# Self-attention of a decoder layer: VectorE turns 32x32 blocks and a round trip through DRAM places them, instead of TensorE transposes; GpSimd forms low halves; scores run two items ahead

## What is computed

```python
k = jnp.einsum('ihd,bpd->biph', W_K, x)
q = jnp.einsum('ihd,bpd->biph', W_Q, x)
v = jnp.einsum('ihd,bpd->biph', W_V, x)
scores = jnp.einsum('biph,biqh->biqp', k, q)
mask = jnp.tril(jnp.ones((pos, pos), dtype=x.dtype))
masked = scores * mask - jnp.float32(10000000000.0) * (1.0 - mask)
attn = jax.nn.softmax(masked / jnp.sqrt(jnp.float32(d_head)), axis=-1)
z = jnp.einsum('biqp,biph->biqh', attn, v)
z_flat = jnp.transpose(z, (0, 2, 1, 3)).reshape(b, pos, -1)
out = jnp.einsum('df,bqf->bqd', W_O, z_flat)
...
xq = activation_quant(rms_norm(x))
g = jax.nn.silu(ternary_matmul(xq, W_g))
u = ternary_matmul(xq, W_u)
p = g * u
return ternary_matmul(p, W_d)
```

## Time and profile before

| | us |
|---|---|
| median of 3 runs | 1622.2 |
| lowest, highest | 1622.14, 1622.71 |
| span of the profiled execution | 1621.2 |
| TensorE busy | 1574.0 (97%) |
| TensorE weight load busy | 1270.9 (78%) |
| VectorE busy | 1014.8 (63%) |
| ScalarE busy | 788.7 (49%) |
| GpSimd busy | 286.4 (18%) |

### The profile page before, as it was taken

One profiled execution on the slowest core, in us unless ns is written; L12 is line 12 of the kernel. 1 busy time (PEld: TensorE's weight loads), 2 busy tenths in 40 slices (PEclk: granted clock), 3 DMA queues, 4 the chain that ended last, 5 costly groups with the idle time before them and its releaser, 6 DMA issues. The chain is left out here.

```text
span 1621.2 us, 25726 instructions
## 1 busy us (share of the span) xinstructions
PE 1574.0 (97%) x8332; PEld 1270.9 (78%) x8352; DVE 1014.8 (63%) x2125; ACT 788.7 (49%) x1789; POOL 286.4 (18%) x301
## 2 busy tenths in 40 slices
PE   8999999999999999999999999997999998999997
PEld 7888888888888888888888888885887775565564
DVE  4555555555555555555555555567899996877854
ACT  5444444444444444444444444444888875433332
POOL 0000000000000000000000000004788872433432
PEclk9999999999999999999999999997999999999998
DMA  5000010100101001010010100011111100000000
GB/s 175 29 31 19 26 32 14 44 19 26 32 13 45 19 26 32 13 42 22 26 32 13 32 32 26 2 45 47 52 58 59 40 20 1 1 27 1 26 26 27
DMA packets 40393, 50.85 MB, mean 31 GB/s; under 512 B 3488, under 2 KB 19872, under 8 KB 40352
## 3 DMA queue, kind: packets, MB, share of 16 engines
q1 hardware_dynamic: 40352, 50.35, 9.7%
HBM read 46.14 MB, written 4.19 MB: 31 GB/s over the span
## 5 line engine op out<-in xcount | busy, mean ns | idle before, releaser
L162 POOL TENSOR_TENSOR norm_rstd<-norm_var_eps,minus_half 128x4 f32<-128x4 f32 x12 | 12.2, 1014 | 1116.2 <-DVE norm_var_eps L122 1116.2
L645 DVE SCALAR_TENSOR_TENSOR acc<-attn_bank,prob_recip,acc 128x512 f32<-128x512 f32 x256 | 179.7, 744 | 16.9 <-PE attn_bank L487 16.9
L510 ACT ACTIVATE probs<-probs,neg_max 128x128 f32<-128x128 f32 (+3 forms) x256 | 142.0, 557 | 61.7 <-DVE neg_max L590 61.7
L581 DVE TENSOR_TENSOR zT_lo<-attn_bank,zT_hi 128x512 fp32r<-128x512 f32 x64 | 44.3, 692 | 190.0 <-ACT zT_hi L504 190.0
L504 ACT CAST kT_hi<-attn_bank 128x512 fp32r<-128x512 f32 x64 | 37.5, 587 | 180.3 <-PE attn_bank L355 180.3
L581 DVE TENSOR_TENSOR qT_lo<-attn_bank,qT_hi 128x512 fp32r<-128x512 f32 x64 | 44.2, 691 | 126.0 <-ACT qT_hi L504 125.9
L581 DVE TENSOR_TENSOR kT_lo<-attn_bank,kT_hi 128x512 fp32r<-128x512 f32 x64 | 44.3, 692 | 122.9 <-ACT kT_hi L504 122.9
L1195 PE MATMUL y_bank<-wdT_f32r,prod_hi 128*128 128x512 f32 x256 | 110.8, 433 | 3.0 <-POOL prod_lo L1136 2.5
L1136 POOL TENSOR_TENSOR prod_lo<-prod,prod_hi 128x512 fp32r<-128x512 f32 x64 | 85.6, 1337 | 142.1 <-ACT prod_hi L1244 142.1
L590 DVE CUSTOM_DVE_ANT_0 probs<-attn_bank,mask 128x128 f32<-128x128 f32 (+3 forms) x256 | 109.8, 485 | 0.1
L487 PE MATMUL attn_bank<-woT_hi,zT_hi 128*128 128x512 f32 x256 | 106.2, 415 | 1.6 <-DVE zT_lo L581 1.4
(11 more groups left out here) (149 smaller groups left out, 4176.1 us busy)
## 6 DMA issues: line engine op xcount, KB each, us to landing
rows_twice<-in_ctx_dram SPq DMA_DIRECT2D x64, 128.0 KB, 2.6
rows<-in_L_attn_W_K_dram SPq DMA_DIRECT2D x16, 256.0 KB, 2.6
rows<-in_L_attn_W_Q_dram SPq DMA_DIRECT2D x16, 256.0 KB, 2.9
rows<-in_L_attn_W_V_dram SPq DMA_DIRECT2D x16, 256.0 KB, 3.4
rows<-in_L_attn_W_O_dram SPq DMA_DIRECT2D x16, 256.0 KB, 2.7
rows_twice<-in_L_ffn_W_g_dram SPq DMA_DIRECT2D x16, 256.0 KB, 2.7
rows_twice<-in_L_ffn_W_u_dram SPq DMA_DIRECT2D x16, 256.0 KB, 2.8
rows_twice<-in_L_ffn_W_d_dram SPq DMA_DIRECT2D x16, 256.0 KB, 2.7
```

What stands on the lines that cost most here:

```text
L510: nc.scalar.activation(probs[:, cols], probs[:, cols], ACT.Exp, bias=low[:, par, t:t + 1], scale=-1.0, accum_out=total[:, par, t:t + 1]).t ...
L581: nc.vector.tensor_tensor(parts[1][:, at:at + cols], bank[:, 0:cols], parts[0][:, at:at + cols].bitcast(F32), ALU.subtract).then_inc(done, 1)
L645: nc.vector.scalar_tensor_tensor(out=acc[:, b * NT + t, :], in0=O_BANK[t][:], scalar=recip[:, par, t:t + 1], in1=acc[:, b * NT + t, :], op ...
```

## The change

TensorE transposes nothing but x at the start. Weights are loaded so that their 32x32 blocks lie already at the right place, and VectorE turns each block (`nc.vector.transpose`, which transposes within 32x32 blocks). For the probabilities and v it turns blocks from SBUF or PSUM into the tile `turned` of 128 x 1792 values (ten blocks of probabilities, four of v). SP stores this tile in a DRAM scratch and loads it again by four DMAs, one for each group of 32 partitions, straight into `pv_lo`; ScalarE casts that to `pv_hi`, and GpSimd subtracts in place. GpSimd also makes the weights' low halves. k, q, scores, mask and v's turn run two items ahead of z and the output (`AHEAD`). The signs go to DRAM and are loaded again in the two later stages, for which the SBUF was taken by the new tiles. x and the quantised x are read by TensorE with a stride of four columns (`chunk_of`).

```diff
+    E, R = 4, 32
+    AHEAD = 2
+    NBLK = NT * (NT + 1) // 2 + NT
+    V_AT = (7, 10, 11, 13)
+    PIECES = ((0, 8), (8, NBLK))
...
+        scratch = [nc.dram_tensor(f"turned_scratch{i}", (P, NBLK, E, R), F32).ap() for i in range(2)]
...
             @block.sync
             def _(sp):
+                def bounce(i, par, first):
+
+                    sp.wait_ge(p_turn, i + 1)
+                    sp.dma_start(scratch[par].rearrange("p n c s -> p (n c s)"), turned[:]).then_inc(written, 16)
+                    sp.wait_ge(written, i * 16 + 16)
+                    if not first:
+                        sp.wait_ge(z_full, i)
+                    for c in range(E):
+                        sp.dma_start(pv[1][c * R:(c + 1) * R, :].bitcast(F32).rearrange("r (n a s) -> r n a s", a=E, s=R),
+                                     scratch[par][:, :, c, :].rearrange("(a r) n s -> r n a s", a=E)).then_inc(landed, 16)
...
+                def step(h, b, last):
+                    if not (last and b == B - 1):
+                        bounce(h * B + b + 1, (b + 1) % 2, False)
+                    if b > 0:
+                        keep_signs(h, b - 1)
+                    if b == 0 and not last:
+                        load_projection(sp, "wk", wk, h + 1)
+                        load_projection(sp, "wq", wq, h + 1)
+                    if b == 1:
+                        wait_apart(sp, k, f_turn, h * 3 + 1)
+                        load_down(sp, h)
+                        if not last:
+                            load_projection(sp, "wv", wv, h + 1)
+                            load_output(sp, h + 1)
...
             @block.gpsimd
             def _(pool):
-                for n in range(B - 2):
-                    norm_gpsimd(nc, pool, norm, k.minus_half, n)
...
+                def pieces_lo(i):
+                    for g, (first, end) in enumerate(PIECES):
+                        cols = slice(first * P, end * P)
+                        pool.wait_ge(pv_hi, i * len(PIECES) + (g + 1))
+                        nc.gpsimd.tensor_tensor(pv[1][:, cols], pv[1][:, cols].bitcast(F32), pv[0][:, cols].bitcast(F32),
+                                                ALU.subtract).then_inc(pv_lo, 1)
...
             @block.scalar
             def _(act):
...
+                def pieces_hi(i):
+                    act.wait_ge(landed, i * (16 * E) + 16 * E)
+                    for first, end in PIECES:
+                        cols = slice(first * P, end * P)
+                        nc.scalar.copy(pv[0][:, cols], pv[1][:, cols].bitcast(F32)).then_inc(pv_hi, 1)
...
                 def step(h, b, last):
-                    more = not (last and b == B - 1)
                     i = h * B + b
...
+                    more = not (last and b + AHEAD >= B)
+                    if not (last and b == B - 1):
+                        exps(i + 1, (b + 1) % 2)
                     if more:
...
+                    if not (last and b == B - 1):
+                        pieces_hi(i + 1)
...
             @block.vector
             def _(dve):
...
+                def turn_probs(i):
+                    for t in range(NT):
+                        dve.wait_ge(exp_done, i * NT + (t + 1))
+                        last = nc.vector.transpose(blocks(turned[:], t, 3, t + 1),
+                                                   blocks(probs[:, s_at[t]:s_at[t] + (t + 1) * P], 0, 1, t + 1))
+                    last.then_inc(p_turn, 1)
+
+                def turn_v(i, first):
+
+                    dve.wait_ge(v_full, i + 1)
+                    if not first:
+                        dve.wait_ge(written, i * 16)
+                    nc.vector.transpose(blocks(turned[:], V_AT[0], V_AT[1] - V_AT[0], 2), blocks(v_bank[:], 0, 1, 2))
+                    nc.vector.transpose(blocks(turned[:], V_AT[2], V_AT[3] - V_AT[2], 2), blocks(v_bank[:], 2, 1, 2)).then_inc(v_turn, 1)
...
                 def step(h, b, last):
-                    more = not (last and b == B - 1)
                     i = h * B + b
                     par = b % 2
+                    more = not (last and b + AHEAD >= B)
+                    if not (last and b == B - 1):
+                        turn_probs(i + 1)
...
+                    if more:
+                        turn_v(i + AHEAD, False)
+                        rows_of_scores(i + AHEAD, par)
```

More of the change, by code:

```diff
@@ L162, in norm_gpsimd, with attention @@
     nc.gpsimd.tensor_tensor(norm.rstd[:], norm.var[:], minus_half[:], ALU.pow).then_inc(norm.rstd_ready, 1)
-def attention(nc, x_in, wk, wq, wv, wo, wg, wu, wd, acc, wT_ffn, rows, k, norm):
-    wd_v = wd.rearrange("(c p) f -> p c f", p=P)
-    gT, uT, dT = wT_ffn
+def attention(nc, x_in, wk, wq, wv, wo, wg, wu, wd, acc, signs, rows, k, norm):
     x_v = x_in.rearrange("b (t p) d -> p (b t) d", p=P)
[L174 to L208, removed]
+    E, R = 4, 32
+    AHEAD = 2
+    ITEMS = H * B
+    BEGIN = ["x0", "x1", "x2", "x3", "k0", "x4", "q0", "x5", "v0", "x6", "x7", "s0",
+             "k1", "x8", "x9", "q1", "x10", "x11", "v1", "x12", "x13", "s1", "x14", "x15"]
     s_at = [sum(P * (u + 1) for u in range(t)) for t in range(NT)]
-    pt_at = [sum(P * (NT - u) for u in range(j)) for j in range(NT)]
     NPAIR = P * NT * (NT + 1) // 2
-    S_BANK = [(0, 0), (0, P), (1, 0), (2, 0)]
-    PT_GROUPS = [(0,), (1,), (2, 3)]
+    NBLK = NT * (NT + 1) // 2 + NT
+    V_AT = (7, 10, 11, 13)
+    PIECES = ((0, 8), (8, NBLK))
     with ExitStack() as ctx:
@@ new lines, in turn_views, with turn_weight @@
+                def turn_views(out, x, chunked):
+                    if not chunked:
+                        return out, x
+                    return out.rearrange("p (a c s) -> p a c s", a=E, c=NC), x.rearrange("p (a r c) -> p a c r", a=E, c=NC)
+                def turn_weight(name, n):
+                    other, before = BEFORE_IN_TMP[name]
+                    if not (isinstance(n, int) and n + before == 1):
+                        dve.wait_ge(w_lo[other], n - 1 + before)
+                    dve.wait_ge(w_loaded[name], n * (16 * E))
+                    nc.vector.transpose(*turn_views(w_turned[TMP[name]][:], raw[name][:], name != "wo")).then_inc(w_turn[name], 1)
@@ L751, in _ @@
             def _(sp):
+                signs.load(sp)
                 def step(b, h):
@@ L1122, in _ @@
             def _(sp):
+                for t in range(NHT):
+                    sp.dma_start(wdT[:, t * D:(t + 1) * D].bitcast(F32), signs.d[:, t * D:(t + 1) * D]).then_inc(wd_loaded[t], 16)
                 with sp.Fori(0, B - 1) as b:
```

606 lines of the change are left out of this document (297 added, 309 removed).

## The result

The changed kernel takes 1761.0 us (1758.5 to 1762.4), the kernel before in the same comparison 1622.2: a ratio of 1.086, interval [1.085, 1.088]. It is 139 us slower. The forecast was 1809 us, the range 1600 to 2050.

What follows compares the result with a forecast made beforehand. The prediction took the detour's chain to bound self-attention, not TensorE: 63 periods of 19.5 us (1228.5), with start, first loads, tail and weights 1297.7, plus 510.6 for later stages and 1.0 to the median: 1809 us, range 1600 to 2050.

Steps and rivals of the forecast that it cites:

- One ring: Self-attention's chain per item: casts of landed blocks, exponentials, last turn, store, four loads; period 19.5 us against TensorE's 14.9.
- Its pieces: Per item: casts 1.8, exponentials 2.3, turn 0.7, store 4.1, load latency 1.8, packets 8.5, hand-offs 0.3 us.
- t: Price of one 128 B packet in the detour's loads, 448 per engine an item: taken as 18.9 ns.
- a line and a flat price: Bounds on a 128 B packet's price: 9.6 ns by a line through 512 B and 2 KB packets, 28.1 ns if flat.
- the sign turns: Packet price of 12.8 ns, a period of 16.7 us, where the time equals that of the kernel before.
- the loads overrun by 0.7 us: Down, value and output weights behind the detour's loads need 5.7 us in a 5.0 us gap: 10 us over 15 heads.
- I leave the start as it is: Item 0's scores were to end at 29.4 us as before, since turning the first weights replaces their transposes.
- The sum: First store's end 35.9, loads 10.3, 63 periods 1228.5, tail 13.0, weights 10, later stages 510.6: 1808.3 us.
- TensorE's clock: Falls to half while TensorE waits at z, returns within the item; rival that it stays low: near 2460 us, chance 0.04.
- The single buffer: The one buffer for landed blocks is free 1.9 us before the next loads want it.
- The DMA share: Busy share of the DMA engines in self-attention, expected near 60% if the forecast was right.
- Cheap packets: Rival: 128 B packets at 9.6 ns, period 15.3 us, time 1531 us, faster than before; chance 0.18.

Runs made afterwards that it cites:

- e11: e3's kernel with one more store of the same 896 KB, to another scratch, written before the loads are issued: 1920.2 us, ratio 1.186.
- e4: Changed kernel with the four loads reading each partition's 7 KB in one run, the placing of blocks left out: 1605.9 us, ratio 0.991 to the kernel before.
- e8: Changed kernel with one load of 128 partitions in 7 KB runs in place of four loads, placing left out: 1552.7 us (one run), ratio 0.958.
- e7: Changed kernel with VectorE instead of GpSimd forming the low halves of the landed blocks: 1789.7 us, ratio 1.104 to the kernel before.
- e3: Changed kernel with v's weights of the next head loaded one item earlier (b = 0): 1688.5 us, ratio 1.041 to the kernel before.
- e1: Changed kernel with ScalarE taking the exponentials of item i+2 before the casts of item i+1: 1929.6 us, ratio 1.189 to the kernel before.

## Why the prediction was right, and where not

- **One ring sets the pace: right, and shown.** Every piece of it stands in the rows above, e11 shows that a longer piece is paid in full, e4 and e8 that its shortening gives TensorE back, e7 that GpSimd, whose row ends TensorE's wait, is not the cause.
- **Its pieces.** Landing to store 4.74 us (forecast 1.8 + 2.3 + 0.7 = 4.8), store 3.6 (4.1), loads 8.6 to 8.7 (10.3), hand-offs in these. Sum 16.9 to 17.1, and 17.4 as the mean of e3's 63 periods, in place of 19.5. TensorE's wait at z is 3.2 us in the row shown, where 4 was forecast; over all items it is 133.0 / 64 = 2.1. The largest error is t: 13.4 to 14.3 ns where I took 18.9, so 2.1 to 2.5 us too much, and what stands beside the packets in the loads took 2.7 us, not 1.8. The interpolated middle between a line and a flat price was too dear; t lay nearer the lower end, and still above the 12.8 ns at which the sign turns, by no more than 0.6 to 1.5 ns. 128 B cost 8.9 GB/s an engine in place of 18.2 at 512 B (14.3 against 28.1 ns), 2.0 times as dear per byte. By the Trainium skill, DMA: Bandwidth & Descriptors, a transfer below 512 B falls short of line rate (section Specifications), with which the trace agrees in direction; the section gives no size. By the 3 cycles a packet of its section Why small descriptors are slow it would be some 1.5 times (an estimate from that page); the rows show more.
- **"In the step with b = 1 the loads overrun by 0.7 us": mis-sized, and the mechanism missed.** I asked whether the packets fit between landing and next store. What is late is v's weights for VectorE, behind which mask and exponentials queue: 4.8 us a head, 72.5 us measured (e3), against 10.
- **"I leave the start as it is": wrong.** The first landing is at 64.16 us, not 46.2. The store of item 0 leaves at 51.83, not near 31.7: its scores end at 41.2 in place of 29.4, since ScalarE's queue is held by the issues of the first weights and TensorE starts 8 us later (rows above), and VectorE turns item 0's probabilities only ahead of item 1's v, at 50.13, after two more groups of x. The loads then take 8.7. What each of these costs by itself was not measured.
- **The sum.** The first landing is 18.0 us late; 63 periods take 1234.52 - 64.16 = 1170.4 us, the waits for v's weights among them, against 1228.5 + 10; the tail to the last add at 1249.4 takes 14.9, not 13.0. So self-attention ends 48 us earlier than forecast (18.0 - 68.1 + 1.9), and 511.0 us follow (forecast 510.6), the signs' reload hidden. The errors go against each other, and that 1809 came within 3% is in part luck: with t at 13.4 to 14.3 ns and nothing else changed the same sum gives 1640 to 1665 us (the weights' loads then fit), some 100 to 120 too low. The wait for v's weights (72.5) and the late start (18) make up most of that.
- **TensorE's clock: right.** It falls at the waits and returns within the item; mean 0.947 in place of 0.987. By the Trainium skill, TensorE: Matmul & The Clock Gate, Part 1, a wait in every round throttles it each time; the rows agree, and in e1 and e11, where TensorE is idle for more of each item, the mean is lower still (0.899, 0.897). In e1 the chain from z to scores, part of it at half clock, is on the path.
- **The single buffer is free in time: right** for this order, but by 0.5 us in the item shown, not by 1.9: z, which starts at half clock, ends 7.8 us after the landing and not 7.0, and the loads leave after 8.3 and not 8.9. A second buffer was not tried by itself in this order, but e11 moves the loads 3.7 us later and still pays in full, which leaves no wait for the buffer.
- **The DMA share was to be near 60%:** the column reads 71 to 75%. A shorter period with cheaper packets doesn't give that; the column counts packets that overlap more than once, and I had reckoned with times that don't.
- **Cheap packets (the rival on the other side): not the case**, but near. Without the wait for v's weights the mean period is 17.4 us (e3) where the forecast had the balance at 16.7, and the kernel 4.1% slower.

## What to carry to other kernels

Taking work off the engine that is the bound pays only if the way round is a shorter chain than what that engine took for an item before; add up the chain through every queue's order and compare it with that and with what the engine keeps. Shorten such a chain by taking out what is ready earlier (here v, 29% of the packets) and by placing loads so that no in-order queue meets them late; before reordering a queue, follow the new order round until it closes, since the ring that it makes can be longer. The engine that ends the wait of another need not be the cause: ask what it waited for itself.

## What the runs showed of the hardware

- A 128 B packet of these DRAM-to-SBUF loads took 14.3 ns of the engines' summed packet times, a 512 B one 28.1. Counted over a stretch in which nothing else ran, it was 13.4 ns of an engine each, while the summed times gave 124% of the stretch: the DMA share in these views isn't bounded by 1.
- The issue of a load of 1792 such runs holds SP's queue for 1.16 us (4.6 to 4.7 us for four), that of a load of 32 runs of 7 KB 0.43 (1.72 for four in e4), that of a store 0.35. On ScalarE's queue, at the start, four loads in runs of 128 B held it for 7.53 us.
- The same 896 KB, read in runs of 7 KB, landed 6.5 us after the first issue as four loads of 32 partitions and 5.0 as one of 128.
- VectorE's 32x32 turn of 128x512 took 1.11 and 1.05 us for the v and up weights, which it reads with a stride of four columns, and 0.70 and 0.67 for the output and down weights, which it reads in order:

```profile
627.25 1.05 DVE L617 STREAM_TRANSPOSE f_turned<-rows_twice 128x512 f32<-128x512 f32 x1
...
638.05 0.70 DVE L612 STREAM_TRANSPOSE w_turned<-rows 128x512 f32<-128x512 f32 x1
638.67 0.67 DVE L617 STREAM_TRANSPOSE f_turned<-rows_twice 128x512 f32<-128x512 f32 x1
```
